# Routed feed forward of the second layer: gather and add thirty of its 32 tiles within the rounds of the next cross attention

## The reference, cut to what matters

```python
def _L1_ffn_ref(x, ...):
    probs = softmax(x_tokens @ router_w + router_b)
    vals, idx = top_k(probs, 2)
    vals = vals / (sum(vals) + 1e-09)
    ...
    expert_outputs = vmap(_mlp)(expert_inputs, w_gate, w_up, w_down)
    gathered = expert_outputs[idx_flat, pos_c] * (vals_flat * within)[:, None]
    return x + _mlp(x, sw_gate, sw_up, sw_down) + gathered.reshape(N, 2, d).sum(axis=1)

x = x + _L1_ffn_ref(_layernorm(x), ...)
x = x + _L2_xattn_ref(_layernorm(x), ctx_1024, W_kv, b_kv, W_o, b_o)   # 16 heads of 8, 257 keys
```

## Time and profile before

| what | value |
|---|---|
| median of 3 timed runs | 5246.27 us (5241.81 to 5249.77) |
| the profiled execution, its own time | 5233.18 us |
| its span, first to last instruction | 5231.3 us |
| granted TensorE clock, mean | 0.937 |
| busy: TensorE, VectorE, ScalarE, GpSimd | 89%, 61%, 41%, 35% |
| tail of the feed forward (first gather's start) | 2625.7 us |
| cross attention, first to last matmul | 2714.8 to about 3260 us |

### The profile page before, as it was taken

The page is one execution under the profiler, slowest core; times in us unless marked ns, Lnnn a source line. Parts: engine busy times, 40 slices in busy tenths (PEclk is TensorE's granted clock), DMA queues, the critical chain, the costliest instruction groups (busy, mean ns, idle before and its releaser), DMA issues.

```text
span 5231.3 us, 141331 instructions
## 1 busy us (share of the span) xinstructions
PE 4657.2 (89%) x50169; PEld 3698.7 (71%) x50169; DVE 3165.2 (61%) x9513; ACT 2156.9 (41%) x5339; POOL 1845.0 (35%) x2796
## 2 busy tenths in 40 slices
PE   4999999989989999895929999778999989988999
PEld 3777777779957777674717777665577768875776
DVE  3777777756546666555426665775466657764443
ACT  1444444422224444341305555332255545543333
POOL 2555555521013333345043443980044434330000
PEclk8999999999989999996959999898899998888999
DMA  6000000000000100001211110002111100005665
GB/s 203 18 18 17 18 18 18 18 2 2 1 17 29 32 28 28 1 0 32 78 50 34 32 32 25 0 0 72 45 35 32 32 17 0 0 0 121 144 143 133
DMA packets 112438, 199.72 MB, mean 38 GB/s; under 512 B 13315, under 2 KB 54659, under 8 KB 111259
## 3 DMA queue, kind: packets, MB, share of 16 engines
q1 hardware_dynamic: 108147, 188.67, 13.8%
q0 software_dynamic: 4096, 8.40, 0.6%
HBM read 183.29 MB, written 18.97 MB: 39 GB/s over the span
## 4 chain that ended last, share of the span: by engine, by line
PE 75%; DVE 7%; issue 6%; ACT 5%; POOL 4%; SPq 1%; DMA 1%; POOLq 1%; DVEq 0%; ACTq 0%
PE psum_banks L555 6%; PE psum_banks L3089 6%; PE psum_banks L3098 5%; PE psum_banks L560 5%; PE psum_banks L620 4%; PE psum_banks L664 4%; PE psum_banks L671 3%; PE psum_banks L1637 3%; PE psum_banks L624 3%; PE psum_banks L1672 2%; PE psum_banks L2117 2%; PE psum_banks L2784 2%; PE psum_banks L1613 2%; ACT scratch L1755 1%; PE psum_banks L2104 1%
## 5 line engine op out<-in xcount | busy, mean ns | idle before, releaser
L787 DVE TENSOR_REDUCE scratch<-psum_banks 128x2 f32<-128x514 f32 x768 | 531.3, 692 | 409.7 <-PE psum_banks L555 405.6
L706 ACT ACTIVATE scratch<-psum_banks 128x512 f32<-128x512 f32 x768 | 458.7, 597 | 489.3 <-PE psum_banks L565 477.5
L560 PE MATMUL psum_banks<-scratch 32*128 32x128 f32 x6144 | 638.5, 309 | 8.1 <-ACT scratch L706 6.1
L555 PE MATMUL psum_banks<-scratch 32*128 32x257 f32 x3072 | 575.3, 440 | 50.1 <-DVE scratch L788 49.9
L560 PEld LDWEIGHTS psum_banks<-scratch 32*128 32x128 f32 x6144 | 475.7, 185 | 17.3 <-ACT scratch L706 8.6
L555 PEld LDWEIGHTS psum_banks<-scratch 32*128 32x128 f32 x3072 | 254.6, 188 | 272.0 <-issue 175.3
L3098 PEld LDWEIGHTS psum_banks<-w_L_ffn_down,scratch 128*128 128x128 f32 (+1 forms) x2560 | 335.6, 193 | 156.2 <-issue 127.5
L3089 PE MATMUL psum_banks<-scratch,w_L_ffn_up 128*128 128x512 f32 (+1 forms) x752 | 381.9, 603 | 8.2 <-DVE scratch L3276 8.2
L3276 DVE TENSOR_TENSOR scratch<-scratch 128x512 f32<-128x512 f32 x304 | 210.3, 692 | 268.3 <-ACT scratch L3142 234.3
L3142 ACT ACTIVATE scratch<-psum_banks 128x512 f32<-128x512 f32 x320 | 190.8, 597 | 430.2 <-PE psum_banks L3089 430.1
L565 PE MATMUL psum_banks<-shift_T,own_batch 32*128 32x128 bf16 x3072 | 350.8, 214 | 0.0
(11 more groups left out here) (496 smaller groups left out, 12268.7 us busy)
## 6 DMA issues: line engine op xcount, KB each, us to landing
scratch<-route_T SPq DMA_DIRECT2D x136, 512.0 KB, 7.4
scratch<-in_ctx SPq DMA_DIRECT2D x99, 514.0 KB, 3.5
scratch<-in_ctx_rows SPq DMA_DIRECT2D x130, 128.0 KB, 2.1
scratch<-route_T SPq DMA_DIRECT2D x8, 1024.0 KB, 8.9
expert_rows<-in_ctx SPq DMA_DIRECT2D x10, 512.0 KB, 17.9
scratch<-expert_rows SPq DMA_DIRECT2D x16, 192.0 KB, 2.7
expert_out<-scratch SPq DMA_DIRECT2D x16, 192.0 KB, 2.1
w_L_ffn_up<-in_L_ffn_up SPq DMA_DIRECT2D x1, 2992.0 KB
```

The source lines that it names most:

```text
L555: return pe.matmul(S[:, g % 2, :], qbd[q, t.odd, (s // 2) * P:(s // 2 + 1) * P], kT_of[q, t.odd, s // 2, :], start=True, stop=True)
L560: return pe.matmul(W[:, g % 2, c * P:(c + 1) * P], kT_of[q, t.odd, b, c * P:(c + 1) * P], qbd[q, t.odd, b * P:(b + 1) * P], start=True, st ...
L706: act.activation(pT[:, b % 2, 2 * h:2 * h + 2].rearrange("p t c q -> p t (c q)"), W, ACT.Exp).then_inc(exp_ready.sem, 1)
L787: dve.tensor_reduce(parts[:, r.t.odd, 2 * h:2 * h + 2, 0, b], S, X_AXIS, ALU.max, negate=True)
```

## The change

The tail keeps tiles 0 and 1: four gathers and four adds. For tiles 2 to 31 the gathers and adds move into the rounds of the cross attention, which is told so by `completes=True`. At the start of round r VectorE copies the weights and row numbers of tile r+3 from the tables to one of two small buffers (`set_rows`; a gather in a loop has to find its row numbers at a fixed address). At the end of round r GpSimd waits for these and for the adds of tile r+1, runs one tiny operation, and issues the two gathers of tile r+3 into one of two buffers (`gather`). At the end of round r VectorE waits for the rows of tile r+2, gathered a round earlier, and adds them to `k.X`, with a wait for itself behind each add (`add_rows`); the statistics of that tile are taken in the next round. Buffers for rows, weights and the table live at the end of the scratch area, where neither stage puts anything else. The loop has 13 iterations instead of 14, and two more rounds are written out.

```diff
+        self.rows_came = self.area[:, SCRATCH - 4 * P:SCRATCH].rearrange("p (t d) -> p t d", t=2)
+        self.rows_at = self.sb("rows_at", [P, 2, 2], U32)
+        self.pair_weights = self.area[:, SCRATCH - 6 * P:SCRATCH - 6 * P + 2 * TILES]
+        self.row_weights = self.area[:, SCRATCH - 5 * P:SCRATCH - 5 * P + 4].rearrange("p (t n) -> p t n", t=2)
+        self.row_carrier = self.area[:, SCRATCH - 5 * P + 4:SCRATCH - 5 * P + 5]
+        self.get_at = self.sb("slots_read", [P, 2 * TILES], U32)
...
-    plan = Plan(3, TILES - 1, TILES + 3, 2)
+    plan = Plan(3, TILES - 3 if completes else TILES - 1, TILES + 3, 2)
...
+    if completes:
+        rows_set, rows_came, completed = PerTile(k.sig("rows_set"), 1), [
+            PerPair(k.plain_sig(f"rows_came_{n}"), 32, TILES // 2) for n in range(2)], PerTile(k.sig("rows_added"), 2)
+        get_no, pair_weights = (t.rearrange("p (n t) -> p n t", n=2) for t in (k.get_at[:, :], k.pair_weights))
...
+        def gather(t):
+            u = t + -2
+            pool.wait_ge(rows_set.sem, rows_set.at(u, 1))
+            pool.wait_ge(completed.sem, completed.at(u + -1, 0))
+            pool.tensor_tensor(k.row_carrier, k.ln_eps[:, :], k.ln_eps[:, :], ALU.add)
+            for n in range(2):
+                pool.indirect_dma_start(k.rows_came[:, t.odd, n * P:(n + 1) * P], None, k.dram["expert_out"],
+                                        bass.IndirectOffsetOnAxis(ap=k.rows_at[:, t.odd, n:n + 1], axis=0)
+                                        ).then_inc(rows_came[t.odd].sem, 16)
...
                 spread(t, 0)
+            if completes and r.third:
+                gather(r.t + 3)
...
+        def set_rows(t):
+            dve.tensor_copy(k.row_weights[:, t.odd, :], pair_weights[:, :, t.index()])
+            dve.tensor_copy(k.rows_at[:, t.odd, :], get_no[:, :, t.index()]).then_inc(rows_set.sem, 1)
+
+        def add_rows(t):
+            u, x = t + -2, k.X[:, t.index(), :]
+            dve.wait_ge(rows_set.sem, rows_set.at(u, 1))
+            dve.wait_ge(rows_came[t.odd].sem, rows_came[t.odd].at(u))
+            for n in range(2):
+                dve.scalar_tensor_tensor(x, k.rows_came[:, t.odd, n * P:(n + 1) * P], k.row_weights[:, t.odd, n:n + 1], x,
+                                         ALU.mult, ALU.add).then_inc(completed.sem, 1)
+                dve.wait_ge(completed.sem, completed.at(u, n + 1))
+
         def one(r):
+            if completes and r.third:
+                set_rows(r.t + 3)
             for s in range(8):
...
+            if completes and r.after and r.own:
+                add_rows(r.t + 2)
...
-        for t in range(TILES):
+        for t in range(2):
             for n in range(2):
                 pool.indirect_dma_start(gathered[:, t, n, :], None, ys, bass.IndirectOffsetOnAxis(ap=get_no[:, n, t:t + 1], axis=0)
-                                        ).then_inc(came[t // 4].sem, 16)
+                                        ).then_inc(came.sem, 16)
...
-        for g in range(groups):
-            dve.wait_ge(came[g].sem, came[g].at(came[g].n))
-            for n in range(2):
-                for t in range(4 * g, 4 * g + 4):
-                    ins = dve.scalar_tensor_tensor(k.X[:, t, :], gathered[:, t, n, :], weights[:, n, t:t + 1], k.X[:, t, :],
-                                                   ALU.mult, ALU.add)
-                link(ins)
+        dve.wait_ge(came.sem, came.at(came.n))
+        for n in range(2):
+            for t in range(2):
+                ins = dve.scalar_tensor_tensor(k.X[:, t, :], gathered[:, t, n, :], weights[:, n, t:t + 1], k.X[:, t, :],
+                                               ALU.mult, ALU.add)
+            link(ins)
```

More of the change, by code:

```diff
@@ L205, in scratch @@
             at += n
-        assert at <= SCRATCH, at
+        assert at <= (SCRATCH - 6 * P if "ctx" in shapes or "carry" in shapes else SCRATCH), at
         return out
@@ L408, in at, with cross_attention @@
         return self.base + n
-def cross_attention(k, q_w, q_b, k_w, k_b, v_w, v_b, o_w, o_b, relu, a):
+def cross_attention(k, q_w, q_b, k_w, k_b, v_w, v_b, o_w, o_b, relu, a, completes=False):
     has_q, has_o = q_w is not None, o_w is not None
@@ L2636, in routed_by_slots @@
         "nm": [P, CT], "rs": [P, CT], "top": [P, 2 * CT], "code": [P, 2 * CT], "w": [P, 2 * CT], "pos": [P, 2 * CT],
-        "inside": [P, 2 * CT], "slot": [P, 2 * CT], "read": [P, 2 * CT], "weights": [P, 2 * TILES]})
-    put_at, get_at = k.sb("slots_written", [P, 2 * TILES], U32), k.sb("slots_read", [P, 2 * TILES], U32)
-    gathered = k.area[:, 0:2 * TILES * P].rearrange("p (t n d) -> p t n d", t=TILES, n=2)
+        "inside": [P, 2 * CT], "slot": [P, 2 * CT], "read": [P, 2 * CT]})
+    put_at, get_at = k.sb("slots_written", [P, 2 * TILES], U32), k.get_at
+    gathered = k.rows_came.rearrange("p t (n d) -> p t n d", n=2)
     up, down = k.load("L1_ffn_up", [P, (E + 1) * W]), k.load("L1_ffn_down", [H, 2 * (E + 1), P])
@@ L2647, in routed_by_slots @@
     top, code, w, pos, inside, slot, read, weights, put_no, get_no = (
-        both(t) for t in (a["top"], a["code"], a["w"], a["pos"], a["inside"], a["slot"], a["read"], a["weights"],
-                          put_at[:, :], get_at[:, :]))
+        both(t) for t in (a["top"], a["code"], a["w"], a["pos"], a["inside"], a["slot"], a["read"],
+                          k.pair_weights, put_at[:, :], get_at[:, :]))
     backwards, pair_no = k.c("expert_backwards"), both(k.c("pair_no"))
@@ L2661, in routed_by_slots @@
     STEPS = 27
-    link_sem = Once(k.sig("vector_step"), 1 + STEPS * CHUNKS + 3 * groups)
+    link_sem = Once(k.sig("vector_step"), 1 + STEPS * CHUNKS + groups + 2)
     var, pool_step, rstd = (Once(k.sig(n), CHUNKS) for n in ("ln_var_ready", "pool_ln_step", "ln_rstd_ready"))
@@ L2674, in routed_by_slots @@
     put_back = [Once(k.sig(f"expert_out_stored_{b}"), 16 * (NU - groups) // 2) for b in range(2)]
-    came = [Once(k.plain_sig(f"gathered_{g}"), 16 * 8) for g in range(groups)]
+    came = Once(k.plain_sig("first_gathered"), 16 * 4)
     def y_read(eng, u):
@@ L3701, in perceiver @@
                 stages.append(cross_attention(k, None, None, "L2_xattn_Wk", "L2_xattn_bk",
-                                              "L2_xattn_Wv", "L2_xattn_bv", "L2_xattn_W_o", "L2_xattn_b_o", False, shared))
+                                              "L2_xattn_Wv", "L2_xattn_bv", "L2_xattn_W_o", "L2_xattn_b_o", False, shared, completes=True))
             if name == "L3_xattn":
```

## The result

| | before | after |
|---|---|---|
| median of 6 timed runs, us | 5247.92 (5241.81 to 5262.64) | 5227.43 (5220.79 to 5228.62) |
| profiled execution, us (span) | 5233.18 (5231.3) | 5226.85 (5225.1) |
| feed forward, second layer, us | 335.0 | 281.2 |
| cross attention, third layer, us | 557.9 | 601.4 |

The ratio is 0.9957, 95% interval 0.9946 to 0.9967: the changed kernel is faster, by 20 us and not by the 69 that were forecast. The lines of before stand further down in the changed file: L505 is L518, L513 L536, L555 L580, L624 L649, L787 L827, L2736 L2779, L2899 L2942. New are L528, a gather within a round, L811, the two additions, and L803 and L804, the two copies.

A forecast was written before the change was run, and what follows sets the result against it. GpSimd's gather issue rate was taken to bound the feed forward's tail, TensorE with VectorE's boundary order the cross attention rounds. Profiled 5233.2 - 75 + 6 = 5164; the 69 us difference carried to timed runs: 5246 - 69 = 5177 us, range 5166 to 5194.

The forecast's parts named there:

- Step 1: End of second layer's feed forward: 60 of 64 gathers leave TensorE's standstill, 1.251 us each, gaining 75 us.
- Step 2: GpSimd at round ends: one tiny operation and two gathers, 2.7 us, fit into 6.1 us of waiting, costing nothing.
- Step 3: Gathered rows in cross attention: land about 2.5 us after issue, needed some 13 us later; two buffers suffice, no cost.
- The fourth rival: Cross attention rounds: gathers starve for descriptors beside busy VectorE, 3.3 us a round, +92 us, 5269 us; chance 0.03.
- The prediction's own sign of being wrong: Cross attention: L513 following a gather without waiting, a gather over 2 us, or span growing over 20 us or not at all.
- Step 4: VectorE's adds and copies at round boundaries: 0.07 us a round plus 0.4 at the back edge, 6 us in all.
- Step 5: Two more cross attention rounds written out instead of looped: 0.3 us gained, in the noise.
- step 6: TensorE's clock after the feed forward pause: 37 us at the low clock before and after, no gain.
- The rule: Skill's rule: VectorE copies can block GpSimd's descriptor writes, about 3.1 us a DMA instead of 0.62; sum about the same.
- the rival of 5269 us: The fourth rival: GpSimd starves in the cross attention rounds, +92 us; chance 0.03.

The follow-up runs named there:

- plain loads: Changed kernel with two plain SyncE transfers a round replacing GpSimd's gathers; 5159.67 us (0.9876 of before) on chip B, 5194.22 us (one run) on C.
- The kernel with the additions alone: Changed kernel without the two gathers of a round and VectorE's wait for them, additions kept; 5178.64 us, 0.9866 of before.
- the kernel with 32 rows: Changed kernel whose gathers in the rounds bring 32 rows instead of 128; 5165.14 us (0.9883 of before) on chip B, 5222.15 us (one run) on C.
- the two apart: Changed kernel with a round's first gather moved behind the spreading of the queries, the second left at the round's end; 5190.71 us, 0.99 of before.

## Why the prediction was wrong

Forecast 5177 us (5166 to 5194), measured 5227. Its steps in order:

**Step 1, 75 us from the standstill: right.** Where both kernels have a profile from one chip the stage is 72.8 us shorter (A, 350.0 to 277.2) and 74.4 (D, 351.8 to 277.4); on chip B it took 260.2, which is 335.0 less 74.8. TensorE's pause went to 17.36 us as written; the first matmul came at 2661 and not at 2640 only because of the scatters ahead.

**Step 2, GpSimd has room: right as far as GpSimd's own time goes.** The operation and the gathers take 2.7 us, as forecast, and L536 then still waits 5.0 us for VectorE (129.8 us in 26 rounds); the longer round makes that more than the 3.4 forecast. Where I put the gathers behind GpSimd's slack instead of into it, the kernel became slower than before: 1.004.

**Step 3, "Each gather brings 64 KB beside one context load of 514 KB a round; no cost": this step failed.** The bytes are indeed free: plain loads of the same size leave the rounds as they were. But I priced a gather only by its bytes and by its time on GpSimd. Its issue also goes with a delay of what other engines do: at the round's end TensorE's dispatch stops twice, for 0.5 to 0.7 us each, and updates of its semaphores arrive 0.4 to 1.4 us late (3.6 to 5.4 us at the line shown in the scatters). At that place TensorE and VectorE hand the score banks back and forth without slack, so the stop goes into the round. How GpSimd's issue does this to TensorE, no run shows. Measured: 561.0 us without gathers, 598.0 to 601.4 with them, 37 to 40 us (and 559.4 to 598.2 on chip D); no rival named it. The fourth rival put a loss on the gathers too, but as GpSimd being late. The prediction's own sign of being wrong, a stage longer by more than 20 us, is what came: 43.5 us (557.9 to 601.4). The evidence was not in the profile that I had, whose scatters show no such delay; it was in the times beside it, 13 us higher. I took that offset for noise that carries over. The later profiles of before, 15.0 and 16.8 us longer in the scatters, say that it was most likely this loss in unchanged code.

**Step 4, VectorE's additions, 6 us: right, and a little high.** They take 1.25 us from the copy of step 7 to the end of L804, and cost 0.29 us at the back edge and nothing in the middle (forecast 0.4 and 0.07), 13 x 0.29 = 4 us. The stage with them took 561.0 us, for 557.9 to 563.0 before. The kernel with the additions alone ran in 5178.64 us, 74 under before; the forecast for the whole was 69.

**Step 5 and step 6: right.** The rounds at the low clock are as many as before (one of 21.9 us and one of 18.9 to 19.3). The granted clock was at its lower level of 0.50 when TensorE began again at 2660.92 and in the whole stretch to 2696, and 0.83 in the next 4 us: 37 us again, after a pause of 17.36 us as after one of 92.15.

**The sum on a chip that doesn't delay.** There the kernel with 32 rows, which makes every instruction of the changed one, took 5165.14 against 5228.17 us: 63 less, 69 forecast. The changed kernel itself did not run on that chip. And a profile of such a run can be short for another reason: in three of the twenty (32 rows and plain loads on B, the two apart on C) the fourth layer's cross attention took 547.4 to 548.0 us instead of 560.0 to 560.3, in unchanged code. I have no cause for these 12 us; the stage lengths that I compare here leave them out.

**Two slips in the sums.** By the terms given for it the range is 5168 to 5193, written as 5166 to 5194; and the fourth rival would cancel the gain from 9.7 us on (69/28 = 2.5 over 7.2), not 9.5. Neither touches the forecast.

**The rule.** The rows first: the gathers beside a busy VectorE took 955 to 1049 ns each, as the scatters did in the median (958), so GpSimd was not starved, and the rival of 5269 us fell. The Trainium skill ("SBUF — State Buffer", "A bandwidth-pool intuition that's wrong") says that contention comes from a port lock or a starved maker of descriptors, not from shared bandwidth. The runs agree for the bytes: with plain loads of the same size the rounds took 16.06 and 16.35 us, as without any. For the rest they show a stall in the other direction: the gathers are on time and the other engines are late.

**Not assigned.** 37 to 40 of the 50 us between forecast and result are the gathers' delay. In the pair of profiles from one chip, D, the spans differ by 27.8 us: 74.4 won and 38.8 lost, and some 7 more lost in stages whose code is the same, 3.1 of them in the stage before the last (413.8 us before, 403.4 in one profile, 416.5 to 417.0 in every kernel with the change). I have no cause for that. And whether chips or something else about a series decides on the delays is open: four series on three chips had them, one series on one chip did not, and no chip had both. The profile of before had none, though its timed runs are as long as those on the three chips. Each time on record has the span and clock of a trace beside it; whether an execution that nobody traces is delayed as well, no run shows.

## What to carry to other kernels

Price an indirect DMA on GpSimd by what its issue does to the engines beside it too, not only by bytes and GpSimd's idle time; put it where the critical loop has slack, and don't put two close behind each other (37 us here against 7). Plain DMAs on SyncE's queue had no such price in this loop. Compare kernels stage by stage and on one chip: the same stage of the same program took 563.0 us in one series and 601.0 in another. Where a profile is 0.25% off its own timed runs, take a second one before you subtract from it.

## What the hardware showed that I had not expected

- In four series on three chips, while GpSimd issued gathers or scatters, semaphore updates of TensorE came 0.3 to 5.4 us late, and beside the second of two gathers TensorE's dispatch stopped, twice a round at the round's end and once in the early place, for 0.5 to 0.7 us with no semaphore involved. The second of two gathers 0.30 us apart costs most: 16.5 us a round with one, 17.5 with two, 16.2 with none.
- In one series, on a fourth chip, none of it occurred, with the same programs: 563.0 us for a stage that took 601.0 elsewhere, and the kernel before was 16 to 25 us faster there.
- It does not depend on the rows gathered: 32 cost what 128 cost (601.0 and 600.7 us for the stage), and both make 32 packets a gather.
